# Narrower score windows for heads 2 to 7 of an attention and mixture-of-experts layer, with a finer proof that the windows are wide enough

## What is computed

```python
slopes = jnp.power(2.0, 8.0 * jnp.arange(0, -H, -1) / H)      # 1, 0.707, 0.5, ... for head 0, 1, 2, ...
scores = jnp.einsum('bhqd,bhkd->bhqk', q, k) / math.sqrt(Hd)
bias = -slopes[:, None, None] * jnp.abs(pos[None, :] - pos[:, None])
probs = softmax(scores + bias[None], axis=-1)
out = jnp.einsum('bhqk,bhkd->bhqd', probs, v)
```

## Time and profile before

| | us |
|---|---|
| median of 3 runs (2243.51 to 2246.77) | 2245.91 |
| the profiled execution's own time | 2257.16 |
| its span | 2255.4 |
| tokens stage, to the first exponential | 302.8 |
| attention, first to last exponential | 1834.5 |
| delivery | 118.2 |

### The profile page before, as it was taken

How to read it: one execution, slowest core, us unless ns; L and a number is a source line. 1 busy time by engine, 2 the same in 40 slices (tenths; PEclk the granted TensorE clock), 3 DMA queues, 4 the chain that set the end, 5 groups by cost and what they waited for, 6 DMA issues and landing times. The chain is left out here.

```text
span 2255.4 us, 41695 instructions
## 1 busy us (share of the span) xinstructions
PE 2005.1 (89%) x16023; PEld 700.9 (31%) x16024; DVE 976.2 (43%) x2318; ACT 1828.7 (81%) x2164; POOL 591.4 (26%) x618
## 2 busy tenths in 40 slices
PE   3989987888889989999999999999999998888888
PEld 1555541111113333333333333333333321111144
DVE  4877657311113443333333443333334434444265
ACT  2878776988988978888988878888988789999911
POOL 1322300355532122222222022222220215544100
PEclk7999999999999999999999999999999999999989
DMA  9667642112133443334334443434335434344356
GB/s 312 219 209 249 217 127 59 41 43 53 45 85 101 107 117 97 113 90 112 97 90 122 110 116 85 113 90 113 100 91 126 107 81 107 106 115 110 107 181 208
DMA packets 195475, 269.01 MB, mean 119 GB/s; under 512 B 82297, under 2 KB 151212, under 8 KB 194748
## 3 DMA queue, kind: packets, MB, share of 16 engines
q1 hardware_dynamic: 157820, 171.63, 27.9%
q0 software_dynamic: 29008, 86.28, 13.0%
q10 hardware_dynamic: 8448, 8.39, 1.1%
HBM read 181.67 MB, written 92.67 MB: 122 GB/s over the span
## 5 line engine op out<-in xcount | busy, mean ns | idle before, releaser
L1331 ACT ACTIVATE probs_att<-SC_att 128x1024 f32<-128x1024 f32 (+10 forms) x1776 | 1584.1, 957 | 174.8 <-PE SC_att L1224 146.5
L1247 PE MATMUL O_att<-probs_att,V_att 128*32 128x512 f32 (+6 forms) x8192 | 931.3, 524 | 16.1 <-DVE probs_att L1357 13.3
L1357 DVE TENSOR_TENSOR probs_att<-probs_att,decay 128x128 f32<-128x128 f32 x1024 | 293.8, 291 | 970.8 <-ACT probs_att L1331 893.7
L1224 PE MATMUL SC_att<-Q,K_turned_att 64*128 64x512 f16 (+7 forms) x2228 | 467.4, 339 | 81.3 <-ACT probs_att L1331 63.5
L1224 PE MATMUL SC_att<-Q,K 64*128 64x512 f16 (+7 forms) x2104 | 425.2, 330 | 59.6 <-ACT probs_att L1331 35.4
L1224 PEld LDWEIGHTS SC_att<-Q,K_turned_att 64*128 64x128 f16 x2228 | 130.0, 92 | 869.2 <-ACT probs_att L1331 580.2
L1172 POOL DMA_DIRECT2D ys<-ys_att x72 | 54.3, 754 | 767.0 <-DVE ys_att L1405 767.0
L1247 PEld LDWEIGHTS O_att<-probs_att,V_att 128*32 128x32 f32 x8192 | 165.2, 108 | 227.9 <-issue 188.1
L1158 POOL DMA_INDIRECT order<-ids_att,place x128 | 123.8, 967 | 224.9 <-ACT probs_att L1331 189.4
L1224 PEld LDWEIGHTS SC_att<-Q,K 64*128 64x128 f16 (+1 forms) x2104 | 125.3, 94 | 155.8 <-ACT probs_att L1331 86.9
L1167 POOL DMA_INDIRECT x<-xn,row_of_att x144 | 139.1, 966 | 127.5 <-PE TY_att L1270 98.5
(11 more groups left out here) (190 smaller groups left out, 1415.4 us busy)
## 6 DMA issues: line engine op xcount, KB each, us to landing
K<-k_stack SPq DMA_DIRECT2D x128, 256.0 KB
Q<-q_stack SPq DMA_DIRECT2D x128, 256.0 KB
ys<-ys_att POOLq DMA_DIRECT2D x72, 256.0 KB
x<-in_x SPq DMA_DIRECT2D x32, 512.0 KB, 5.9
k_stack<-inverse SPq DMA_DIRECT2D x96, 128.0 KB
q_stack<-inverse SPq DMA_DIRECT2D x96, 128.0 KB
xn<-x_tok SPq DMA_DIRECT2D x16, 512.0 KB, 5.8
values<-v_block_tok SPq DMA_DIRECT2D x16, 512.0 KB, 5.3
```

Source lines behind the costliest of these rows:

```text
L1224: mm = pe.matmul(SC[:, c % SLOTS, at:at + x1 - x0], K[par][side or 0][rows, k * P:(k + 1) * P], Q[par][rows, x0:x1], start=True, stop=True)
L1247: mm = pe.matmul(O[VW * g:VW * (g + 1), par, col:col + width * len(mine)], V[par][:, k, :], spans[:, j0:j0 + BPB * (len(mine) - 1) + 1:BPB ...
L1331: nc.scalar.activation(probs[chunk.step % DEPTH][:, chunk.base:chunk.base + chunk.width], SC[:, c % SLOTS, start:start + chunk.width], ACT ...
L1357: v.tensor_tensor(diag, diag, decay[:, chunk.head, :], ALU.mult).then_inc(faded, 1)
```

## The change

Three things are edited.

1. `REACH` goes from seven entries to eight, and six heads get narrower windows. Head 7, which had none, gets one, and with it the 64-column blocks of `block_of`.

| head | reach before, after | chunks a batch | columns a batch |
|---|---|---|---|
| 2 | 384, 256 | 16, 16 | 12,800, 9,472 |
| 3 | 512, 384 | 24, 16 | 15,872, 12,800 |
| 4 | 768, 512 | 28, 24 | 21,248, 15,872 |
| 5 | 1024, 704 | 32, 28 | 25,600, 19,968 |
| 6 | 1472, 960 | 32, 32 | 30,720, 24,576 |
| 7 | none, 1344 | 32, 32 | 32,768, 29,568 |
| all 16 | | 444, 428 | 418,304, 391,552 |

Heads 0 (8 chunks), 1 (16 chunks, 9,472 columns, reach 256) and 8 to 15 (32 chunks, 32,768 columns each) keep theirs. Steps stay at 248 and diagonal blocks at 256 a batch.

2. The proof is made for each pair of 128-token tiles that lies beyond the reach, with the distance of that pair, rather than with the maxima of a whole batch. `largest` keeps 4 maxima a block, `pair` has 64 numbers a row, `limit` is a 16x16 table for each head, and the 8 operations of `guard` work on 16 partitions of 1024 elements. They are taken one a chunk from head 5 of batch 1 instead of all at once at head 6. Their operands lie in unused parts of the buffer `o`.

3. The whole-batch maxima on DVE (a reduction and a memset), the buffer and the semaphore `peaked` go, and `limit` is loaded with the routing's constants.

The numbers `ROUTE_FROM`, `PREFIX_AT` and `ORDER_AT` and all percentages stay. Multiples of a batch's columns shrink with it: the steps that can take a part of an expert tile go from 477 to 436, the first part from chunk 370 to chunk 360 of batch 0, and the last from chunk 144 (head 6) to chunk 148 (head 7) of batch 3.

```diff
-REACH = (192, 256, 384, 512, 768, 1024, 1472)
+REACH = (192, 256, 256, 384, 512, 704, 960, 1344)
...
-    limit = np.full((H, B), 2.0 ** 42, np.float32)
+    limit = np.full((H, KT, KT), 2.0 ** 42, np.float32)
+    tiles_off = np.abs(np.arange(KT)[:, None] - np.arange(KT)[None])
     for h, reach in enumerate(REACH):
-        limit[h] = slope[h] * reach - UNDER - 1
+        away = np.maximum(reach + 1, (tiles_off - 1) * P + 1)
+        limit[h] = np.where(tiles_off * P > reach, slope[h] * away - UNDER - 1, limit[h])
...
-                        for dst, src in ((keep["turn"], a["turn"]), (keep["decay"], a["decay"]), (keep["limit"], a["limit"])):
+                        for dst, src in ((keep["turn"], a["turn"]), (keep["decay"], a["decay"])):
...
-                    v.tensor_reduce(stat[0:3 * VW, j:j + 1], GU[0:3 * VW, 2, :], AX.X, ALU.max).then_inc(own_read, 1)
+                    v.tensor_reduce(stat[0:3 * VW, j, :], GU[0:3 * VW, 2, :].rearrange("p (t n) -> p t n", n=P), AX.X, ALU.max).then_inc(own_read, 1)
...
-        route_loads = [(lower[:], a["lower"]), (starts[:], a["starts"]), (lane[:], a["lane"]), (ids[:], a["ids"]),
+        route_loads = [(limit, a["limit"]), (lower[:], a["lower"]), (starts[:], a["starts"]), (lane[:], a["lane"]), (ids[:], a["ids"]),
...
-                sp.wait_ge(peaked, 1)
-                sp.dma_start(keep["stats"], peaks[:]).then_inc(peaks_out, 16)
+                sp.dma_start(keep["stats"], keep["stat"][0:3 * VW].rearrange("p j t -> p (j t)")).then_inc(peaks_out, 16)
...
+                    wide = [H, B, KT, KT]
+                    of_query = lambda n: pair[:, n].unsqueeze(3).broadcast_to(wide)
+                    of_key = lambda n: pair[:, n].unsqueeze(2).broadcast_to(wide)
                     dve.wait_ge(peaks_in, 48)
-                    steps(v.tensor_tensor(room[:], limit[:], pair[:, 2, :], ALU.subtract))
-                    steps(v.tensor_tensor(pair[:, 0, :], pair[:, 0, :], pair[:, 1, :], ALU.mult))
...
+                    steps(v.tensor_tensor(room, limit.unsqueeze(1).broadcast_to(wide), of_query(2), ALU.subtract))
+                    yield
+                    steps(v.tensor_tensor(product, of_query(0), of_key(1), ALU.mult))
+                    yield
...
-                v.tensor_reduce(peaks[0:3 * VW, :], keep["stat"][0:3 * VW, :].rearrange("p (b g) -> p b g", b=B), AX.X, ALU.max)
-                v.memset(peaks[3 * VW:P, :], 0.0).then_inc(peaked, 1)
...
-                        if i == half and h == 6 and b == 1:
-                            guard()
+                        if b == 1 and h >= 5:
+                            next(guarding, None)
```

More of the change, by code:

```diff
@@ L1005, in attend_stage @@
         r = Room(nc, ctx, "att", keep)
-        Q, V_raw, decay, turn, limit, ident = (keep[n] for n in ("Q", "V_raw", "decay", "turn", "limit", "ident"))
+        Q, V_raw, decay, turn, ident = (keep[n] for n in ("Q", "V_raw", "decay", "turn", "ident"))
         K = [[keep["K"][n], r.sb(f"K{n}_turned", [P, S], F16)] for n in range(2)]
@@ L1012, in attend_stage @@
         least, most = keep["least"], keep["most"]
-        peaks = r.sb("peaks", [P, B])
-        pair = r.sb("pair", [H, 3, B])
-        room = r.sb("room", [H, B])
+        limit = keep["o"][0:H, 3, 1, 0:KT * KT].rearrange("p (i k) -> p i k", k=KT)
+        pair = keep["o"][0:H, 3, 1, KT * KT:KT * KT + 3 * B * KT].rearrange("p (n b t) -> p n b t", n=3, b=B)
+        room, product, square = (keep["o"][0:H, n].rearrange("p c n -> p (c n)").rearrange("p (b i k) -> p b i k", b=B, k=KT) for n in range(3))
         within = keep["within"]
@@ L1417, in guard @@
                 def guard():
+                    wide = [H, B, KT, KT]
+                    of_query = lambda n: pair[:, n].unsqueeze(3).broadcast_to(wide)
+                    of_key = lambda n: pair[:, n].unsqueeze(2).broadcast_to(wide)
                     dve.wait_ge(peaks_in, 48)
[L1419 to L1426 removed]
+                    steps(v.tensor_tensor(room, limit.unsqueeze(1).broadcast_to(wide), of_query(2), ALU.subtract))
+                    yield
+                    steps(v.tensor_tensor(product, of_query(0), of_key(1), ALU.mult))
+                    yield
+                    steps(v.tensor_scalar(product, product, 1.05, None, ALU.mult))
+                    yield
+                    steps(v.tensor_tensor(square, room, room, ALU.mult))
+                    yield
+                    steps(v.tensor_tensor(product, product, square, ALU.is_le))
+                    yield
+                    steps(v.tensor_scalar(room, room, 0.0, None, ALU.is_ge))
+                    yield
+                    steps(v.tensor_tensor(product, product, room, ALU.mult))
+                    yield
+                    steps(v.tensor_reduce(within[:], product.rearrange("p b i k -> p (b i k)"), AX.X, ALU.min))
                     steps.end()
@@ L1529, in route @@
                     at.end()
-                dve.wait_ge(consts_in, 48)
+                dve.wait_ge(consts_in, 32)
                 turn_k(0)
@@ L1538, in _ @@
                     stage_v(n)
-                routing = route()
+                routing, guarding = route(), guard()
                 v.memset(least[:], 1.0)
@@ L2893, in build @@
                 "turn": pass_on("turn", [P, 1]),
-                "limit": pass_on("limit", [H, B]),
                 "ident": pass_on("ident", [P, P]),
```

11 lines of the change are left out of this document (4 added, 7 removed).

## The result

| | before | after |
|---|---|---|
| median (4 runs each) | 2246.34 us | 2190.12 us |
| lowest to highest | 2243.51 to 2249.81 | 2186.09 to 2192.08 |
| the profiled execution's own time | 2257.16 | 2189.79 |
| attention, first to last exponential | 1834.5 | 1762.7 |
| tokens stage / delivery | 302.8 / 118.2 | 305.4 / 120.1 |

The ratio is 0.9747 (0.9727 to 0.9766): the change saves 56 us by the medians. The forecast was 89 us, and 2157 lay well outside what was measured. Between the two profiled executions the saving is 67 us.

A forecast was written before the change was run, and what follows sets the result against it. Attention was taken as a chain of ACT exponentials with small holes. Windows 97.2 less routing 3, proof 3 and first tile 2 gave 89.2: profiled 2257.2 to 2168, less 11.3 to the median, 2157 us; range 2135 to 2182.

The forecast's parts named there:

- The windows: Heads 2 to 7: narrower shapes, priced from batch 0's head times, save 24.3 us a batch, 97.2 in four.
- clock rival: DVE's stretches, reciprocals, proof and first tile lower PE's clock: four or five more falls at 3.3 us, about 2172; chance 0.17.
- The expert parts: All 288 parts on fewer steps, moving from narrow to wide heads: no cost, 2 us either way a batch possible.
- The sign that the forecast gave for being wrong: Untouched heads 8 to 15 taking much more than 35.7 us each would mean the expert parts stand too dense.
- The proof: Eight larger DVE operations in head 5 of batch 1, 8.7 us: loses 3 us, bounds 0 and 8.7.
- The routing: Batch 0, chunks 64 to 91 (head 4), where DVE bounds: loses 3 us of the saving, bounds 0 and 6.
- The first tile: First expert part at chunk 360 of batch 0: PE waits for its tokens, loses 2 us once, bounds 0 and 5.
- The median: Profiled execution lies 11.3 us above the median of the runs; the same difference turns 2168 into 2156.7.
- PE is the bound: Rival: PE limits the attention, saving 12.3 us a batch, 49 in all, less 8: 2205; chance 0.08 for 2185 to 2215.
- The average rate: Rival: columns saved at attention's average rate, 117 us less 8 is 109, so 2137; chance 0.13 for 2120 to 2140.
- the general path: Rival: proof fails at `redo` in `deliver_stage` and the general path runs as well, 3910 us or more; chance 0.01.

The follow-up runs named there:

- dense_before: Kernel before with its expert parts packed onto 437 steps instead of 477, no column removed: 2208.95 against 2204.98 us, ratio 1.0012.
- proof_only: Kernel after with the old seven-entry REACH, so the finer proof alone: 2267.31 against 2261.64 us for the kernel before, ratio 1.0028.
- four_moved: Kernel after with the three small moves, plus the routing from chunk 108 (head 6) instead of 64: 2196.08 us, ratio 0.9754 to before; repeated, 0.9732.
- order_early: Kernel after with the sorted list turned round at chunks 336 and 342 instead of 350 and 356: 2145.77 us, ratio 0.9736 to before.
- three small moves: Kernel after with earlier list turning, reciprocals at head 8, proof operations every fourth chunk from head 9 of batch 1: 2131.09 us, ratio 0.9665 to before; repeated, 0.9656.
- no_tiles_recips_late: Kernel after without expert tiles and mixing, and with the reciprocals at head 8 instead of head 4: 1987.22 us (one run).

## Why the prediction was wrong, step by step

**The account.** On the quiet chips the change saved 2204.98 − 2145.77 = 59 us (with the order early) and 2206.06 − 2146.46 = 60 us. Without the tiles it saved 74. The forecast's sum splits the same way: 91.2 for windows, routing and proof, and −2 for what hangs on the tiles. So the first part was 17 to 18 us too high, and what hangs on the tiles took some 14 in place of 2.

**The windows (97.2): the step that failed.** The mechanism was right: 1712 exponentials, head 2 at 11.0 and head 3 at 12.75 us in every batch, as the shapes say. The size was not. Two things were wrong in it:

- *"32,768 columns 32.90", and the interpolation from it.* Batch 0's heads 5 to 7 were taken as free of other work because they have no expert part. Head 5 holds the second half of the routing, and heads 6 and 7 have the sorting beside them, which goes with up to 3 us a head on that chip. The clean prices are 22.5, 25.99, 28.67 and 29.89 for the old heads 4 to 7. Head 4 gives 22.5 − 18.65 = 3.8 in place of 5.0, head 6 3.2 in place of 4.6, head 7 2.0 in place of 2.3. With 0.7 and 0.2 more from heads 2 and 5 the price is 22.3 us a batch with the reciprocals away, in place of 24.3: 8 us in all.
- *Head 4, a term that was missing.* The reciprocals cost 3.7, 2.8 and 2.7 us among narrower chunks, 9.2 us in all by the runs without tiles. With 1.0 us more for batch 1's proof than forecast (head 5 there takes 24.62 against 20.62), half a microsecond less for the routing, and as much lost in heads 2 and 3 of batches 1 and 3, that is the 18 that were missing. The forecast had the reciprocals in its clock rival only, with the sign right (head 4 of the kernel after has clocks of 0.94 and 0.93 in batches 2 and 3), and bought them no place in the sum. So the windows' term of 97.2 us measured some 80: 89.2 by clean prices, less 9.2 for the reciprocals.

**The expert parts (0): mis-sized.** The forecast's prices from 0.71 down to 0.29 us a part stood on batch 0's heads. From clean heads a part costs (35.72 − 29.96)/9.6 = 0.60 us in heads 8 to 15 of the earlier trace rows, twice the 0.29 used, and (22.28 − 18.63)/5 = 0.73 in head 3. After the change the wide heads pay (36.55 − 29.96)/10.6 = 0.62. The forecast's claim was another, that the move of parts is neutral. It splits by batch:

| tiles' cost, us | batch 1 before, after | batch 2 before, after |
|---|---|---|
| heads 2 to 7 (41, then 34 parts) | 166.07 − 138.45 = 27.6, 145.42 − 124.12 = 21.3 | 164.43 − 138.46 = 26.0, 147.01 − 118.92 = 28.1 |
| heads 8 to 15 (77, then 85 parts) | 285.75, 292.16: +6.4 | 284.56, 292.43: +7.9 |

In batch 1 the touched heads give back 6.3 and the others take 6.4: neutral, as forecast. In batch 2 the touched heads give back nothing for 7 parts less, since each part got dearer there: 26.0/41 = 0.63 us before, 28.1/34 = 0.83 after. Head 4 pays 4.9 us for 5 parts (26.34 against 21.42), and its clock is 0.94; with the reciprocals at head 8 it pays 3.3. In batch 3 it is the other way: heads 2 to 7 go from 22.9 for 28 parts to 19.4 for 27. Over the three batches a part of the touched heads costs the same, 76.5/110 = 0.70 us before and 68.8/95 = 0.72 after, and one of heads 8 to 15 goes from 90.9/155 = 0.59 to 105.3/170 = 0.62. The sign that the forecast gave for being wrong, heads 8 to 15 above 35.7, was met: 36.5 a head in both batches. Of the 12 us by the medians dense_before shows some 3 as the price of closeness alone. So the move was not neutral: heads 8 to 15 of batches 1 and 2 took 14.3 us, and heads 2 to 7 of batches 1 to 3 gave back 7.7. Why the rest of those 12 us arises was not separated.

**The proof (3).** 4.6 in head 5 with its clock, some 6 by proof_only (interval 2.3 to 10.2). The operations' prices were right. The cover was put too high, 5.7 us where 4.0 were hidden; the fall of the clock was named as a possible extra.

**The routing (3).** Near in size, a little high. Heads 4 and 5 of batch 0 went from 61.9 to 54.0, so they saved 7.9. Clean, and without reciprocals, these heads save (22.47 − 18.65) + (25.99 − 20.62) = 9.2, so 1.3 were lost; by heads 2 to 7 of batch 0 (19.8 against 22.3) it was 2.5. The stretch of chunks 64 to 91 takes 32.95 us after and 34.17 before: it nearly keeps its time, as said.

```profile
354.73:387.68 32.95, 19.51 (x29) 0.79 0.18 43
```

Wrong was that this stretch holds the whole routing: it holds 28 of 55 pieces. That wide chunks carry such work better, as four_moved expected, did not hold on the two chips that ran it.

**The first tile (2).** The kernel after, in order of time:

```profile
661.58 0.95 POOL L1168 DMA_INDIRECT x<-xn,row_of_att  x1 [0.30 <-issue]
...
661.82 0.97 PE L1271 MATMUL TY_att<-ident,x 128*128 128x128 f32 x4 [2.49 <-DMA x<-xn,row_of_att]
...
663.36 1.02 ACT L1332 ACTIVATE probs_att<-SC_att 128x1024 f32<-128x1024 f32 x1 [2.97 <-PE SC_att L1225]
```

PE waits 2.5 us for the tokens, and ACT 3.0 behind it. Forecast were a wait of 3 to 4 and 2 us on the path; order_early got 2.5 back in that head, though not visibly by its ratio.

**The median.** The forecast subtracted 11.3 us as a constant. It was most likely the scatter of one execution: the kernel after's own profiled execution, 2189.79, stood on its median.

**The rivals.** "PE is the bound" (2205) came nearest in time, with the measured 2190 inside its 2185 to 2215, and was right for two thirds among the tiles. It failed for heads without tiles, and batch 2's 11.7 us against its 12.3 is chance: the touched heads gave 19.5 and the others took 7.9. "The clock" (2172) named two of the true losses, head 4 and the proof, at 3 to 5 us each, and came 18 us short. The average rate and the general path had nothing for them.

## What to carry to other kernels

A price taken from a stretch with one kind of side work is not clean because another kind is absent: take the side work out of the kernel once, read the base there, and only then price what each piece adds. When chunks get narrower, try another place for the fixed work that is threaded between them: three small moves gave back 15 us together, and each new place has to be measured, as the fourth shows. Use one execution's distance from its median as scatter, not as an offset.

## What the runs showed of the hardware

The same program differs by up to 2.7% between chips (2205 to 2265 us for the kernel before), and the ratios hardly do (0.9723 to 0.9747 for the kernel after). The difference stands where POOL's indirect transfers for the sorting and the mixing run. The attention of the kernel after took 1762.7 us in the result's profile and 1720.9 on a quiet chip; of these 41.8 us batch 0, with the sorting, has 27.1, batch 3, with the mixing, 11.7, and batches 1 and 2 have 1.5 each. Batch 0's head 9 took 29.97 us on quiet chips, with ACT busy for all of it, and 34.1 us in the result's execution at the same clock of 1.0. Without tiles, on a chip that is not quiet (no_tiles_recips_late), the same head 9 is long in batch 0 and clean in batch 1, which has no sorting:

```profile
494.84:529.21 34.37, 30.52 (x33) 1.00 0.20 49
890.69:920.67 29.98, 29.98 (x33) 1.00 0.19 45
```

What in the chip makes that difference is not known from these runs. And on the two chips that ran it, a late chain of POOL's transfers went along with 30 us in which PE was busy for 10 to 13 and ACT for 8, at a clock of 0.50, with no wait in the records that would explain it.
